# Reordering two engines in an expert loop: GpSimd's gather before its scatter, VectorE's shared-expert additions before its gating

## The reference

```
xn  = layernorm(X)
# attention-like branch
Xn2 = layernorm(xn) * gamma + beta
Q, K, V = split(Xn2 @ W_in + b_in);  K, V = rotary(K), rotary(V)
A   = 0.5 * sum over tokens of cos_sim(K) * cos_sim(V) + 0.5     # one row per batch
att = (A * Q) @ W_out + b_out + xn
# mixture of experts, 16 experts, top 4, at most 128 tokens an expert
scores = softmax(xn @ gate_w.T);  top 4, weights scaled to sum 1
for each expert e: rows xg = xn[its tokens]
    mid  = silu(xg @ w_gate[e]) * (xg @ w_up[e])                 # 176 wide
    y[its tokens] += (mid @ w_down[e]) * weight
shared = (silu(xn @ sw_gate) * (xn @ sw_up)) @ sw_down           # 352 wide
out = X + att + y + shared
```

## Time and profile before

| | |
|---|---|
| runs | 202.39, 202.94, 201.33 us; median 202.39 |
| profiled execution | 202.58 us |
| its span, first to last instruction | 200.8 us |
| busy, TensorE matmul | 172.8 us (86%) |
| busy, TensorE weight load | 141.0 us (70%) |
| busy, VectorE | 105.3 us (52%) |
| busy, ScalarE | 76.7 us (38%) |
| busy, GpSimd | 112.2 us (56%) |
| mean granted TensorE clock | 0.906 of full speed |

### The profile page before, as it was taken

How to read it: one execution, slowest core, us unless ns; L and a number is a source line. 1 busy time by engine, 2 the same in 40 slices (tenths; PEclk the granted TensorE clock), 3 DMA queues, 4 the chain that set the end, 5 groups by cost and what they waited for, 6 DMA issues and landing times.

```text
span 200.8 us, 3157 instructions
## 1 busy us (share of the span) xinstructions
PE 172.8 (86%) x1017; PEld 141.0 (70%) x1017; DVE 105.3 (52%) x303; ACT 76.7 (38%) x228; POOL 112.2 (56%) x134
## 2 busy tenths in 40 slices
PE   6939999999468989969996897999979999999910
PEld 5539498998266867947875686777958778879900
DVE  0666169877972245052584146653643564308691
ACT  0042234767615978243665122363231433320000
POOL 2567138993600523961897788759827684320380
PEclk9975559999859999978999699999999999999985
DMA  6999980220079120651556355555517332224968
GB/s 191 367 376 405 359 272 13 95 104 5 0 166 303 44 74 1 164 137 33 129 148 158 51 142 146 130 108 146 132 38 165 114 56 26 26 26 62 303 227 275
DMA packets 25172, 28.69 MB, mean 143 GB/s; under 512 B 4034, under 2 KB 23971, under 8 KB 25124
## 3 DMA queue, kind: packets, MB, share of 16 engines
q1 hardware_dynamic: 21650, 23.75, 36.8%
q0 software_dynamic: 3072, 4.33, 12.8%
q10 hardware_dynamic: 434, 0.41, 0.6%
HBM read 21.79 MB, written 8.79 MB: 152 GB/s over the span
## 4 chain that ended last, share of the span: by engine, by line
PE 67%; DVE 12%; POOL 7%; issue 6%; ACT 3%; DMA 2%; DVEq 1%; ACTq 0%; POOLq 0%
PE bank L229 14%; PE bank L230 12%; PE bank L231 12%; PE bank L988 9%; PE bank L999 3%; PE bank L836 3%; PE bank L998 2%; POOL ysum L364 2%; DVE xn_all L830 2%; DMA xg<-rows,idx 2%; PE bank L1021 2%; PE bank L975 2%; DVE xn_all L737 2%; PE bank L863 2%; PE bank L841 1%
## 5 line engine op out<-in xcount | busy, mean ns | idle before, releaser
L364 POOL DMA_INDIRECT ysum<-eo,idx x16 | 30.5, 1908 | 29.4 <-ACT eo L532 26.9
L229 PE MATMUL bank<-wkvr_s,xt_all 128*128 128x256 f32 (+1 forms) x96 | 31.6, 329 | 3.4 <-DVE wkvr_s L685 3.1
L231 PE MATMUL bank<-wkvr_s,xt_all 128*128 128x256 f32 (+1 forms) x96 | 29.3, 306 | 0.0
L230 PE MATMUL bank<-wkvr_s,xt_all 128*128 128x256 f32 (+1 forms) x96 | 29.2, 304 | 0.0
L988 PE MATMUL bank<-xgt,wgu 128*128 128x128 f32 (+1 forms) x192 | 24.9, 281 | 0.6 <-issue 0.6
L356 POOL DMA_INDIRECT xg<-rows,idx x16 | 16.1, 1008 | 16.5 <-issue 16.5
L229 PE MATMUL bank<-xt_all,sw_s 128*128 128x512 f32 (+1 forms) x48 | 20.5, 427 | 4.1 <-DVE xn_all L737 4.1
L229 PEld LDWEIGHTS bank<-wkvr_s,xt_all 128*128 128x128 f32 x96 | 20.2, 210 | 5.1 <-DVE xt_all L599 3.4
L988 PEld LDWEIGHTS bank<-xgt,wgu 128*128 128x128 f32 (+1 forms) x192 | 23.1, 192 | 0.8 <-issue 0.8
L230 PEld LDWEIGHTS bank<-wkvr_s,xt_all 128*128 128x128 f32 x96 | 20.4, 213 | 0.0
L231 PEld LDWEIGHTS bank<-wkvr_s,xt_all 128*128 128x128 f32 x96 | 20.2, 210 | 0.0
(11 more groups left out here) (147 smaller groups left out, 372.8 us busy)
## 6 DMA issues: line engine op xcount, KB each, us to landing
wgu<-in_w_gu SPq DMA_DIRECT2D x16, 368.0 KB
rows<-xn_all SPq DMA_DIRECT2D x4, 512.0 KB, 4.0
wdn<-in_w_dn SPq DMA_DIRECT2D x16, 128.0 KB
x_all<-ysum SPq DMA_DIRECT2D x4, 512.0 KB, 6.9
x_all<-in_x SPq DMA_DIRECT2D x3, 512.0 KB, 7.5
out<-xn_all SPq DMA_DIRECT2D x3, 512.0 KB, 3.2
trg<-in_trig SPq DMA_DIRECT2D x1, 1024.0 KB, 8.1
wdn<-in_w_dn SPq DMA_DIRECT2D x16, 48.0 KB
```

Source lines behind the costliest of these rows:

```text
L229: nc.tensor.matmul(dst, lt_hi, r_hi, start=start, stop=False)
L230: nc.tensor.matmul(dst, lt_hi, r_lo, start=False, stop=False)
L231: return nc.tensor.matmul(dst, lt_lo, r_hi, start=False, stop=stop)
L364: nc.gpsimd.indirect_dma_start(out=ysum, out_offset=bass.IndirectOffsetOnAxis(ap=idx[:, e:e + 1], axis=0), in_=eo[:, e % G, :], in_offset= ...
```

## The change

In GpSimd's slot the gather is called ahead of the scatter. In VectorE's slot `keep` is called first of all, ahead of `columns`, `mix_lo`, `shared_mid` and `gated`, instead of behind `shared_lo`. No instruction, wait or size changes.

```diff
@@ GpSimd @@
             for e in range(E):
                 if e in WEIGHTS:
                     weights(WEIGHTS[e])
+                if e + 3 < E:
+                    gather(e + 3)
                 if e:
                     scatter(e - 1)
-                if e + 3 < E:
-                    gather(e + 3)
                 for i in KEYS[e]:
                     rotate(i)
             scatter(E - 1)
@@ VectorE @@
             for e in range(E):
                 units = FILL[e - 1] if e else ()
                 now = [3 * u[1] + u[2] for u in units if u[0] == "S"]
+                for u in units:
+                    if u[0] == "D":
+                        keep(u[1], u[2])
                 if e - 1 in SUMS:
                     columns(SUMS[e - 1], e - 1)
                 if e - 2 in SUMS:
...
                 gated(e)
                 for q in now if e else [1]:
                     shared_lo(q)
-                for u in units:
-                    if u[0] == "D":
-                        keep(u[1], u[2])
                 for i in KEYS[e]:
                     products(i)
                 for i in KEYS[e - 1] if e else ():
```

## The result

The changed kernel took 196.14 us (median; 194.99 to 198.88), the kernel before 202.27 us beside it. The ratio is 0.9699, with a 95% interval of 0.9655 to 0.9743: 3.0% faster. The forecast was 196.3 us.

What follows compares the result with a forecast made beforehand. TensorE's own work and what holds it up were taken to bound the kernel. Gains of 5.67 and 3.66 us, together 9.3, less 3.0 given back, leave 6.3: 202.58 - 6.3 = 196.3 us, range 193.4 to 200.2.

Steps and rivals of the forecast that it cites:

- Part 1: VectorE adds first: TensorE's holds in slots 2, 7 and 11 and slot 2's low clock go, 5.67 us.
- The cover: Slot 2's two additions, 1.29 us, run under the gate and up matmuls, so `gated` isn't delayed.
- Part 2: GpSimd gathers first: slot 6's hold for gather(7) shrinks by 1.98 us and its low clock goes, 3.66 us.
- the pair of DMAs takes the same time in either order: GpSimd's gather and scatter take as long together when swapped, so `rotate` behind them starts as before.
- What is given back: In or just ahead of slot 8, late GpSimd holds TensorE 2.0 us, plus 1.0 us low clock: 3.0 us.
- the term that was left open: GpSimd's scatter(4) waits 0 to 1.6 us for scatter(3) to land, delaying gather(9) as much.
- The clock term: Slot 8's hold, above the 1.64 us after which the clock fell, adds 1.0 us, between nothing and 1.68.
- the term of slot 2: Slot 2 gains 3.19 us: the 1.64 us hold and 1.55 us of lower clock behind it.
- Rival C: Scatter chain limits: a gather ahead adds 3.70 us to each landing; 3.4 to 11.5 us slower, 210 us; chance 0.06.
- the prediction's estimate: By the pipelining rule a scatter behind a gather pays its bytes, 0.3 us for 139 KB: 196.6 us.
- Rival B: GpSimd keeps up, token sums hardly held: gain 8.1 or the whole 9.3 us, say 194.0 us; chance 0.14.
- rival D: Slower rotations and scatter(4)'s wait hold token sums 2.8 us, longer low clock, or slot 2's stays: 199.4 us; chance 0.20.

Runs made afterwards that it cites:

- e4: Changed kernel with VectorE's additions of slots 7 and 11 back in their old place: 197.64 us.
- e10: The changed kernel once more, unchanged: 196.36 us.
- e1: Kernel before with only VectorE's additions moved, GpSimd keeping its old order: 197.58 us.
- e9: Changed kernel with GpSimd's rotations ahead of the scatter and only the token weights of tiles 12 to 15 moved, from slot 6 to 10: 192.53 us.
- e5: Changed kernel with GpSimd's rotations ahead of the scatter (gather, rotations, scatter): 193.21 us.
- e3: Changed kernel with GpSimd's token weights of tiles 8 to 11 in slot 7 and of tiles 12 to 15 in slot 10: 195.69 us.
- e2: Kernel before with only GpSimd's gathers moved ahead, VectorE keeping its old order: ratio 0.9884, median of all seven executions 201.77 us.
- e11: The same program as e2, once more, unchanged: a stage of 98.95 us against 101.79 in e2.
- e8: Changed kernel with GpSimd's order rotations, scatter, gather, and token weights of tiles 8 to 15 late, in slots 7 and 10: 202.36 us.
- e7: Changed kernel with only slot 2's two additions back in their old place: 202.1 us.
- e12: The same program as e7, once more and timed: 197.87 us.

## Why the prediction was right

**Part 1, the additions.** Slot 2: 3.19 us predicted, 3.22 measured. Slot 11: 1.44 and 1.47. Slot 7's 1.04 us can't be seen alone after the change, since the hold for gather(9) ends the same slot; e4 brought it back at 1.04. The cover held: `gated` in slot 2 still waited for silu. That nobody waits for `keep` in slots 6 and 15 held too. That nobody waits for it at all held in the first profile only: in e10 0.73 us of slot 7's wait were there again. Taken alone part 1 gave 4.2 us of stage and not 5.7; here the prediction had no term, because it walked the two parts together only, and e1 showed the 1.30 us hold for gather(9).

**Part 2, the gathers.** Hold for gather(7): 0.50 us predicted, 0.28 measured (0.48 in e10). Low clock of slot 6: 1.68 us predicted, 1.62 measured. That the pair of DMAs takes the same time in either order was right in some slots alone. Before, the first rotation behind scatter(3) and gather(7), which GpSimd's timeline of the kernel before has as

```profile
108.57 0.74 POOL L381 TENSOR_TENSOR home_b<-home_b,trg 128x256 f32<-128x256 f32 x1
```

ended at 109.31, 3.71 us after the scatter's start at 105.60. In the kernel after, in slot 1:

```profile
79.03 1.02 POOL L356 DMA_INDIRECT xg<-rows,idx  x1 [2.10 <-ACT eo L532]
80.35 1.63 POOL L364 DMA_INDIRECT ysum<-eo,idx  x1 [0.30 <-issue]
81.43 1.32 POOL L381 TENSOR_TENSOR home_b<-home_b,trg 128x256 f32<-128x256 f32 x1
```

The rotation now starts 0.55 us before the scatter's issue ends, but takes 1.32 us instead of 0.74: it ends at 82.75, 3.72 us after the gather's start. But in the slots that lead to slot 8 the same stretch, from the start of the pair to the end of the first rotation, got longer: 4.27 against 3.71 us in slot 4, 3.92 against 3.68 in slot 5, 4.37 against 3.88 in slot 6. GpSimd's timeline of slot 4:

```profile
101.43 1.04 POOL L356 DMA_INDIRECT xg<-rows,idx  x1 [0.20 <-issue]
102.78 2.15 POOL L364 DMA_INDIRECT ysum<-eo,idx  x1 [0.30 <-ACT eo L532]
104.40 1.30 POOL L381 TENSOR_TENSOR home_b<-home_b,trg 128x256 f32<-128x256 f32 x1
```

**What is given back.** Predicted 3.0 us. Measured, with e9 for the slots without a hold: 7.18 - 5.60 = 1.58 us in slot 7 and 8.07 - 6.64 = 1.43 in slot 8, 3.0 us. The place was right, and that it is GpSimd's lateness, as e5 and e9 show: put its work in another order and take some of it away, and nothing is left. (e3 alone moved it, from the gathers to the token sums.) Why GpSimd was so late was not right: the term that was left open, a wait of scatter(4) for a landing of 0 to 1.6 us, was 0.3 us at most (0.56 us idle before the scatter, where 0.30 are usual), and the longer pairs and token weights (1.38 against 1.07 us in slot 6) stood in its place. So gather(9) started 11.20 us after gather(7), within the 9.96 to 11.56 of the walk. The two terms in the 3.0 us were not right either. I had 2.0 us of holds and 1.0 us of low clock; there were 2.42 us of holds, no low clock, and 0.6 us that stand in no single row. The hold for gather(9) was put at 0 to 1.1 us and was 1.42: its issue took 1.69 us, against 1.01 for gather(7) before, and it landed 4.4 us after its start instead of 3.70. Before, no gather took more than 1.23 us to issue; in the new order, where it goes first, the longest took 2.48 us. Why isn't shown. The clock term rested on the wrong idea that a longer hold decides, with 1.64 us as a price list. e2 and e11 show that it does not: the same program and the same hold give either level. In the changed kernel 1.42 and 1.80 us left the clock whole, and in e8 2.02 us did. Behind the 1.64 us hold of slot 2 the clock was low in four of five profiles (before, e2, e7, e12; not e11). So the 1.55 us in the term of slot 2 are what most of these executions lose, and a part of the forecast's agreement is luck. So is it that the first and the last stage, which were to stay unchanged, moved by 0.95 and 0.78 us in opposite directions.

**The signs.** Two of the signs that were named came out against it. TensorE's wait for a gather was to be under 1 us, and it was 1.42 us (1.80 in e10); and "TensorE waiting for gathers in slots 8 and later" was to show that the prediction is wrong, while just this wait opened slot 8. The walk itself had allowed 0 to 1.1 us for it.

**The rule and the rivals.** Rival C asked for scatters to land 3.70 us later behind a gather. Line 364 of the kernel after, against the earlier trace rows:

```profile
DMA to landing us min/median/max: 3.7/3.8/4.7
```

They land as before, and the 0.3 us more of the prediction's estimate aren't in the medians (3.9 and 3.8). This agrees with the rule of the Trainium skill ("DMA: Bandwidth & Descriptors", section "Two DMAs through the same engine are not ordered") that descriptors of one queue start in order but are pipelined. Where C came nearest is e3, when GpSimd had less to do: a single step of 6.86 us from one scatter to the next. Rival B's gain, 8.1 to 9.3 us, was there only with further edits: 9.1 us of stage in e5, 10.0 in e9. Of rival D, the slower rotations are in the trace (behind the scatter the first operation takes 1.3 us instead of 0.74), and a longer hold with a longer low clock in e7 alone, whose slot 2 isn't that of the change.

## What to carry to other kernels

When a hold is removed, walk each other engine's queue forward from there and ask who is late next: here 3.0 of some 9.5 us that were freed (6.5 of stage and these 3.0) went to the next queue, and the walk found the place, and the size in sum. In a queue that runs in order, put first what others wait for, and last what only waits: the gather first, then the rotations, and the scatter, which waits for the landing of the one before it, last. Judge a small change by the stretch of the trace that it touches: the stages around it, which weren't changed, differed by up to 3 us between executions.

## What the runs showed of the hardware

The clock behind a short hold isn't a function of the hold. In or just ahead of slot 8 it fell behind 0.63 us (e2), 0.94 us (e4), 1.92 us (e7), 2.07 us (e8) and 2.15 us (e3), and stayed whole behind 0.59 us (e11), 1.34 and 0.33 us (e12), 1.42 and 1.00 us (after), and 1.80 and 0.77 us (e10). In slot 2 1.64 us did either. At the start of slot 5 it stayed whole behind 2.02 us (e8); at the start of slot 6 it fell behind 2.48 us (before) and 2.52 us (e1). A fall cost 1.4 to 3.0 us. The Trainium skill ("TensorE: Matmul & The Clock Gate", section "Part 1: The HAM clock gate (the "warmup" mystery)") says that where the clock changes is variable between runs of one kernel, as the chip's watch over the engine runs by itself and isn't started by the kernel. That the place varies, e2 and e11 show; the reason no run here can show.

An indirect DMA followed by a vector operation and one followed by another indirect DMA aren't the same for GpSimd. The rotation behind a scatter started 1.08 us after the scatter's start (80.35 and 81.43 above), the gather behind a scatter 1.93 us after it; but the rotation then took 0.58 us longer, so nothing was won in slot 1, and in slots 4 to 6 the whole stretch was 0.2 to 0.6 us longer.
